# Attention scores on four 32-row groups of TensorE, with the products of two jobs in turn

## The chip, the cores and the metric

The kernel runs on one core of one Trainium2 chip. The metric is the device time of one execution in microseconds (us). All work is in one program: TensorE (PE), VectorE (DVE), ScalarE (ACT), GpSimd (POOL) and SyncE (SP, which only issues DMAs here) each run their own list in order and wait for each other through semaphores.

## The reference

A decoder layer on 16 samples of 128 tokens with 128 features, with a context of 77 tokens per sample, and a linear attention behind it:

```
x = layernorm1(x + mha(x, x, x, mask))         # 16 heads of 8 features, mask 128 x 128
x = layernorm2(x + mha(x, ctx, ctx, no mask))  # 77 keys
x = layernorm3(x + relu(x @ w1 + b1) @ w2 + b2)   # 512 hidden features
# linear attention over ctx
q, k = elu(x), elu(ctx)
x = layernorm(x + (q @ (k^T ctx)) / (q . sum(k) + 1e-6))

mha: scores = q k^T / sqrt(8); where mask == 0: -1e9; softmax over keys; times v; output projection
```

## The kernel before, in words

**Jobs and slots.** A job is one attention (self "s" or cross "c") of one sample; there are 32. Samples go in groups of two (G = 2), eight groups. `run_iterations` unrolls twelve iterations, and `iteration` has four slots k = 0 to 3 per iteration: a group's self attention jobs are at k = 0 and 1, its cross attention jobs, one iteration later, at k = 2 and 3. `schedule(i, k)` names for each slot the current job `cur`, the next one `nxt`, the previous one `prev`, and `prev_y` before that. The feed-forward part of a group runs two iterations after its self attention and the linear attention with it (`TAIL`); these and the projections are the `light_work` of a slot, placed by the table `PROJ_USES` as (name, stage, k, place), two PSUM banks in turn (`bank_of`). A bank is opened for a new use only when the last use was read (`open_bank`).

**Scores.** Queries and keys are split into a high and a low bf16 part. A head has 8 features, and 4 combinations of high and low, so 32 rows of contraction. The scores of a job are computed twice: query-major (`query_major`, L412, queries on the partitions) to find each row's maximum, and key-major (`key_major`, L439, keys on the partitions) for the exp, whose output feeds the product with the values. Each is done in two halves h of eight heads. Here two heads (JJ = 2) share 64 rows: the array `wide` holds the queries twice, each time with the other head's rows zero (the zeros are set once by two memsets on POOL, L1118). With 64 rows per instruction two row groups r = 0, 1 are in use, each with its own bank: `s1_ps[r]` for query-major, `s2_ps[r]` for key-major. A query-major half has 8 matmuls, a key-major half 4 of 256 columns. For self attention, `add_bias` (L403) first writes the mask into both banks with 4 matmuls of 64 x 64. After the key-major products, 4 matmuls subtract the maximum (L460), whose transposed bf16 parts come from `split_max` (DVE), `transpose_max` (PE) and `widen_max` (DVE, L920).

**Order around it on TensorE** (`iteration`, L650), in each slot: second half of the values product of `prev` (`times_v`, L478), `query_major(nxt, 0)`, `key_major(cur, 0)`, light work at place 0, `post_transpose_pv` of `prev` (L489), light work 1, `query_major(nxt, 1)`, `post_transpose_att` of `prev` (L494), `key_major(cur, 1)`, `post_project` of `prev` (L498), light work 2, first half of `times_v` of `cur`, `transpose_max` of `nxt`, light work 3 and 4. `blanks` are filler matmuls in the last iterations, `keep_busy` in the first.

**What it waits for.** `query_major` waits for the spreads of its rows (DMA) and, at h = 0, for the widened maximum of the job before, which shares a bank with the transposed maximum; at each half for the maxima read by DVE (`max_bank`, L904). `key_major` waits for the exp of the half before in its banks (`exp_bank`, ACT, L723). `post_transpose_att` waits for `normalise` (DVE, L934), `post_project` for ACT's copy `copy_att` (L734). ACT's order in a slot is `copy_av`, exp of bank 0, light work 0 (among it `scale_y`, L745), exp of bank 1, light work 1, `copy_att`, the two exps of half 1, light work 2 to 4. DVE's: `standardise`, two maxima, light work 0, `normalise`, light work 1, two maxima, `split_max`, `residual`, light work 2, `statistics`, `widen_max`, light work 3 and 4.

**Rows to the groups.** `spread_q_rows` (L291) issues 8 DMAs per group and kind on SP's queue (some of the last group on ACT's); `spread_k` issues 4. At the start SP also issues `late_loads` (L346) behind the first spread: inputs of the second group, the rows of biases, x, and the last weights (`w_rest`), for which TensorE waits at the start of iteration 0 (L652).

## Time and profile before

| | |
|---|---|
| runs | 295.7, 296.0, 297.46 us; median 296.0 |
| profiled execution | 296.44 us, span 294.6 us |
| granted TensorE clock, mean over the span | 0.955 |
| busy, share of the span | PE 254.7 us (86%), DVE 192.1 (65%), ACT 153.4 (52%), POOL 113.5 (39%) |
| TensorE weight loads | 159.4 us (54%), beside the matmuls |

The span is from the first to the last instruction of the program. Busy is the union of the times of an engine's instructions; matmuls are pipelined and their ends are modelled, so the start of the next instruction tells more than the duration of one. A row of the timeline is: start in us from the span's start, busy us, engine, line, operation, out<-in, shapes, count of instructions merged, and in brackets the idle time of the engine before it and what ended it. "Query-major" rows are L428, "key-major" rows L450.

### The profile page before, as it was taken

What the parts mean: (1) busy time and instruction counts of PE and PEld (TensorE: products, weight loads), DVE (VectorE), ACT (ScalarE), POOL (GpSimd) and SP (SyncE); (2) the same over time, 40 slices, a digit from 0 to 9 for tenths busy, and PEclk for the clock granted to TensorE, in tenths of its full rate; (3) what the DMA queues carried; (4) which work ended last, traced back from release to release, by engine and by line L of the source; (5) the groups of instructions that cost most, each with busy time, mean ns of one, the idle gap of its engine ahead of it and who ended that gap; (6) DMA issues with size and microseconds to landing.
All of it is one profiled execution on the core that took longest, in us unless ns stands there. A gap on an engine that the chain in (4) does not pass through costs nothing.

```text
span 294.6 us, 8333 instructions
## 1 busy us (share of the span) xinstructions
PE 254.7 (86%) x3036; PEld 159.4 (54%) x3036; DVE 192.1 (65%) x606; ACT 153.4 (52%) x374; POOL 113.5 (39%) x222
## 2 busy tenths in 40 slices
PE   8959678899998989999999999999998979779880
PEld 4424344555576557655765576557655746455540
DVE  7055355678848984898489848984898454554324
ACT  3004413565748565856585658565856563345520
POOL 5020230043224354535453545354535452632471
PEclk9997956999999999999999999999999986999998
DMA  4390111221220132012201220112010001000000
GB/s 128 93 274 7 47 49 33 75 57 44 83 59 18 33 86 76 18 33 80 79 20 36 80 77 18 36 49 80 18 36 20 19 14 37 2 29 2 0 18 19
DMA packets 28624, 14.61 MB, mean 50 GB/s; under 512 B 8024, under 2 KB 28200, under 8 KB 28584
## 3 DMA queue, kind: packets, MB, share of 16 engines
q1 hardware_dynamic: 27256, 13.48, 16.2%
q10 hardware_dynamic: 1328, 0.60, 0.7%
q8 instruction: 24, 0.39, 0.5%
q14 instruction: 16, 0.13, 0.2%
HBM read 5.46 MB, written 1.05 MB: 22 GB/s over the span
## 4 chain that ended last, share of the span: by engine, by line
PE 62%; DVE 19%; issue 6%; SPq 4%; POOL 3%; DMA 3%; ACT 2%; POOLq 0%; DVEq 0%; ACTq 0%
PE av_ps L478 10%; PE proj_ps L508 9%; DVE neg_max L904 7%; PE s_ps L408 6%; PE proj_ps L562 5%; PE s_ps L450 5%; PE s_ps L428 5%; PE post_ps L498 4%; PE s_ps L460 3%; SPq L295 3%; PE post_ps L494 3%; PE s_ps L396 3%; DMA w_sb<-in_weights 2%; DVE att L934 2%; PE proj_ps L521 2%
## 5 line engine op out<-in xcount | busy, mean ns | idle before, releaser
L723 ACT ACTIVATE probs<-s_ps 128x512 f32<-128x512 f32 (+1 forms) x128 | 72.0, 592 | 53.9 <-PE s_ps L460 53.9
L904 DVE TENSOR_REDUCE neg_max<-s_ps 128x4 f32<-128x512 f32 (+1 forms) x128 | 68.4, 576 | 36.6 <-PE s_ps L428 36.6
L1140 POOL TENSOR_SCALAR var_e<-mv 128x1 f32<-128x1 f32 x32 | 7.2, 224 | 99.9 <-DVE mv L955 99.9
L396 PE MATMUL s_ps<-zeros_b 128*128 128x512 bf16 x96 | 25.6, 398 | 1.0 <-POOL zeros_b L1115 1.0
L729 ACT COPY av_sb<-av_ps 128x256 f32<-128x256 f32 x32 | 11.7, 365 | 26.0 <-PE av_ps L478 25.9
L460 PE MATMUL s_ps<-max_x,unit_sel 64*128 64x256 bf16 (+1 forms) x256 | 25.2, 276 | 0.0
L508 PE MATMUL proj_ps<-x_t,w_sb 128*128 128x256 f32 (+1 forms) x80 | 21.8, 391 | 0.7 <-issue 0.6
L408 PE MATMUL s_ps<-bias_q,id_b 64*64 64x512 bf16 x128 | 14.2, 431 | 9.2 <-DVE neg_max L904 3.7
L1149 POOL TENSOR_TENSOR y_g<-y_n,row_sb 128x128 f32<-128x128 f32 x32 | 14.6, 458 | 17.3 <-DVE y_n L961 17.3
L478 PE MATMUL av_ps<-probs,v_aug_c 77*32 77x128 f32 x512 | 21.3, 288 | 0.0
L920 DVE TENSOR_TENSOR max_x<-s_ps,max_is_j 128x256 bf16<-128x256 bf16 x32 | 13.6, 425 | 11.4 <-PE s_ps L437 11.4
L478 PE MATMUL av_ps<-probs,v_aug_s 128*32 128x128 f32 x512 | 20.6, 279 | 0.2 <-ACT probs L723 0.2
L1142 POOL TENSOR_TENSOR rstd<-var_e,neg_half 128x1 f32<-128x1 f32 x32 | 18.2, 568 | 2.7
L494 PE MATMUL post_ps<-id_f,att 128*128 128x128 f32 x32 | 10.6, 333 | 8.3 <-DVE att L934 8.2
L745 ACT ACTIVATE x_t<-proj_ps,col_sb 128x128 f32<-128x128 f32 x32 | 14.4, 451 | 6.2 <-PE proj_ps L578 6.2
L776 ACT ACTIVATE hid<-proj_ps,col_sb 128x256 f32<-128x256 f32 (+1 forms) x32 | 12.9, 458 | 8.8 <-PE proj_ps L508 8.8
L562 PE MATMUL proj_ps<-w_sb,hid 128*128 128x128 f32 x120 | 16.6, 281 | 0.6 <-ACT hid L776 0.4
L498 PE MATMUL post_ps<-w_sb,att_t 128*128 128x128 f32 x64 | 16.1, 335 | 1.0 <-ACT att_t L734 1.0
L946 DVE TENSOR_TENSOR x_post<-post_ps,r 128x128 f32<-128x128 f32 x32 | 9.2, 288 | 11.2 <-PE post_ps L498 10.4
L562 PEld LDWEIGHTS proj_ps<-w_sb,hid 128*128 128x128 f32 x120 | 15.1, 191 | 2.5 <-ACT hid L776 2.1
L478 PEld LDWEIGHTS av_ps<-probs,v_aug_s 128*32 128x32 f32 x512 | 12.0, 109 | 6.6 <-issue 4.3
L1151 POOL TENSOR_TENSOR r<-y_g,res_bias 128x128 f32<-128x128 f32 x32 | 14.6, 456 | 2.5
(121 smaller groups left out, 505.3 us busy)
## 6 DMA issues: line engine op xcount, KB each, us to landing
xt_in<-in_x_t SPq DMA_DIRECT2D x8, 128.0 KB, 2.3
sq_wide<-sq_hi SPq DMA_DIRECT2D x32, 32.0 KB, 2.3
sq_wide<-sq_lo SPq DMA_DIRECT2D x32, 32.0 KB, 1.9
x_all<-in_x SPq DMA_DIRECT2D x8, 128.0 KB, 2.2
cq_wide<-cq_lo SPq DMA_DIRECT2D x32, 32.0 KB, 1.9
out<-o_all SPq DMA_DIRECT2D x8, 128.0 KB, 1.9
sk_rows<-sk_hi SPq DMA_DIRECT2D x14, 64.0 KB, 1.9
sk_rows<-sk_lo SPq DMA_DIRECT2D x14, 64.0 KB, 1.9
```

The lines of the kernel that those rows point to most:

```text
L396: nc.tensor.matmul(bank[:, :], zeros_b[:], zeros_b[:].unsqueeze(1).to_broadcast([P, RH, S]), start=True, stop=True, skip_group_check=True)
L408: nc.tensor.matmul(banks[r][RP * c:RP * (c + 1), :], id_b[rows, rows], bias[rows, int(c != r), :].unsqueeze(1).to_broadcast([RP, RH, S]), ...
L428: last = nc.tensor.matmul(s1_ps[r][:, at:at + n], wide[kind][rows, g % 2, jj, u, b, :], rows_k[kind][rows, g % K_COPIES[kind], u, b, :], s ...
L460: last = nc.tensor.matmul(s2_ps[r][0:n, uu * JJ * S:(uu + 1) * JJ * S], unit_sel[rows, u, 0:n], max_x[rows, b, :, :], start=False, stop=Tr ...
L478: last = nc.tensor.matmul(av_ps[32 * r:32 * r + VW, rr * S:(rr + 1) * S], v_aug[kind][:, b, u, r, :], probs[0:KLEN[kind], half, r // JJ, r ...
L494: nc.tensor.transpose(post_ps[:, 2, :], att[:, b, :], id_f[:]).then_inc(M["attt_ps"], 1)
L498: nc.tensor.matmul(post_ps[:, 3, :], att_t[:, b, :], w_sb[:, W_SO if kind == "s" else W_CO, :], start=True, stop=True).then_inc(M["o_ready ...
L508: return nc.tensor.matmul(bank[:, at:at + n], w_sb[:, w, :], src, start=True, stop=True)
L562: last = nc.tensor.matmul(bank[:, b * D:(b + 1) * D], hid[:, c, b, :], w_sb[:, W_2 + c, :], start=(c == 0 and b == first_b(i)), stop=(c == ...
L723: nc.scalar.activation(probs[0:n, h, r, :, :, :].rearrange("p u j n -> p (u j n)"), s2_ps[r][0:n, :], ACT.Exp, scale=SCALE).then_inc(M["ex ...
L904: nc.vector.tensor_reduce(neg_max[:, b, r, RH * h:RH * (h + 1)], scores, AX_X, ALU.max, negate=True).then_inc(M["max_done"], 1)
L1142: nc.gpsimd.tensor_tensor(rstd[:, b, :], var_e[:, b, :], neg_half[:, 0:1], ALU.pow).then_inc(M["rstd_ready"], 1)
```

## The change

- `rows_q` takes the place of `wide`: each head has its own 32 rows (HR = 32), there are no zero rows, no memsets on POOL and no wait for them. Weights are permuted on the host to suit (`order`).
- A spread of queries is 4 DMAs instead of 8, of 64 KB instead of 32 KB.
- A half is now 8 query-major matmuls of 32 rows (as before in number) and 8 key-major ones of 32 rows and 128 columns (4 of 64 rows and 256 columns before), and 8 matmuls of 128 columns that subtract the maximum (4 of 256 before). Half h of query-major takes row groups h and 2 + h, half h of key-major the other two.
- `score_half` opens both (waits and biases first), issues the query-major matmuls of `nxt` and the key-major ones of `cur` in turn, and then subtracts the maximum of `cur`.
- The order in TensorE's slot changes: `score_half(0)`, `post_transpose_pv`, light work 0, 1 and 2, `score_half(1)`, `post_transpose_att`, `post_project`, `times_v` of `cur`, `transpose_max`, light work 3 and 4. "la" moves from place 2 to place 3 of slot 3.
- `widen_max` is a plain copy of 128 columns instead of a product of 256.
- The sum behind the feed-forward part (L1041) moves ahead of the maxima in DVE's slot 2.
- The wait for `w_rest` moves from the start of iteration 0 to its slot 3; the first filler has 22 matmuls instead of 28.

```diff
-                for jj in range(JJ):
-                    eng.dma_start(
-                        wide[kind][4 * jj + s:P:8, g % 2, jj, :, :, :].rearrange("p u b n -> p u (b n)"),
-                        part_of(kind + "q", s)[jj * RP:(jj + 1) * RP, :, :].rearrange("p b n -> p (b n)")
-                    ).then_inc(M[f"spread_{kind}q"], 16)
+                eng.dma_start(rows_q[kind][s:P:4, g % 2, :, :, :].rearrange("p u b n -> p u (b n)"),
+                              part_of(kind + "q", s)[:].rearrange("p b n -> p (b n)")).then_inc(
+                    M[f"spread_{kind}q"], 16)
...
+            def head_rows(r, odd):
+
+                return slice(HR * (2 * r + odd), HR * (2 * r + odd + 1))
+
+            def open_query_major(kind, b, g, job, h):
+
                 if h == 0:
                     wait_spread(pe, kind + "q", g)
                     wait_spread(pe, kind + "k", g)
...
                 wait_reuse(pe, M["max_done"], job * UNITS + RG * h)
                 if kind == "s":
                     add_bias(s1_ps, bias_q)
+
+            def open_key_major(kind, b, g, job, h):
+
+                wait_reuse(pe, M["exp_done"], job * UNITS + RG * h)
+                if kind == "s":
+                    add_bias(s2_ps, bias_k)
+
+            def query_major(kind, b, g, job, h, u, r):
+
+                n = KLEN[kind]
+                rows = head_rows(r, h)
+                last = nc.tensor.matmul(s1_ps[r][:, u * n:(u + 1) * n], rows_q[kind][rows, g % 2, u, b, :],
+                                        rows_k[kind][rows, g % K_COPIES[kind], u, b, :],
+                                        start=(kind == "c"), stop=True, skip_group_check=True)
+                if u == UNITS - 1:
+                    last.then_inc(M["s1_ready"], 1)
+
+            def key_major(kind, b, g, job, h, u, r):
+
+                rows = head_rows(r, 1 - h)
+                nc.tensor.matmul(s2_ps[r][0:KLEN[kind], u * S:(u + 1) * S], rows_k[kind][rows, g % K_COPIES[kind], u, b, :],
+                                 rows_q[kind][rows, g % 2, u, b, :],
+                                 start=(kind == "c" and u == 0), stop=False, skip_group_check=True)
+
+            def subtract_max(kind, b, g, job, h):
+
+                if h == 0:
+                    pe.wait_ge(M["maxt_ready"], job + 1)
+                for u in range(UNITS):
+                    for r in range(RG):
+                        rows = head_rows(r, 1 - h)
+                        last = nc.tensor.matmul(s2_ps[r][0:KLEN[kind], u * S:(u + 1) * S],
+                                                unit_sel[rows, u, 0:KLEN[kind]], max_x[rows, b, :],
+                                                start=False, stop=True, skip_group_check=True)
+                        if u == UNITS - 1:
+                            last.then_inc(M["s2_ready"], 1)
+
+            def score_half(nxt, cur, h):
+
+                if nxt:
+                    open_query_major(*nxt, h)
+                if cur:
+                    open_key_major(*cur, h)
+                for u in range(UNITS):
+                    for r in range(RG):
+                        if nxt:
+                            query_major(*nxt, h, u, r)
+                        if cur:
+                            key_major(*cur, h, u, r)
+                if cur:
+                    subtract_max(*cur, h)
...
             def iteration(i):
-                if static(i) and i == SELF:
-                    pe.wait_ge(M["w_rest"], 16)
                 for k in range(4):
+                    if static(i) and (i, k) == (SELF, 3):
+                        pe.wait_ge(M["w_rest"], 16)
                     cur, nxt, prev, _ = schedule(i, k)
                     if static(i) and i == NEXT and k == 3:
...
-                        keep_busy(28)
+                        keep_busy(22)
                     if prev:
                         times_v(i, *prev, 1)
                     blanks(i, k, "scores")
-                    if nxt:
-                        query_major(*nxt, 0)
-                    if cur:
-                        key_major(*cur, 0)
-                    blanks(i, k, "y")
-                    light_work(i, k, 0)
+                    score_half(nxt, cur, 0)
                     blanks(i, k, "pv")
                     if prev:
                         post_transpose_pv(*prev)
+                    blanks(i, k, "y")
+                    light_work(i, k, 0)
                     light_work(i, k, 1)
...
-                    if nxt:
-                        query_major(*nxt, 1)
+                    light_work(i, k, 2)
+                    score_half(nxt, cur, 1)
...
                     if prev:
                         post_transpose_att(*prev)
-                    if cur:
-                        key_major(*cur, 1)
                     blanks(i, k, "proj")
                     if prev:
                         post_project(*prev)
...
-                    light_work(i, k, 2)
                     if cur:
                         times_v(i, *cur, 0)
...
-                nc.vector.tensor_tensor(max_x[:, b, :, :], nmt_ps.unsqueeze(1).to_broadcast([P, JJ, S]),
-                                        max_is_j[:].unsqueeze(2).to_broadcast([P, JJ, S]), ALU.mult).then_inc(
-                    M["maxt_ready"], 1)
+                nc.vector.tensor_copy(max_x[:, b, :], nmt_ps).then_inc(M["maxt_ready"], 1)
```

## Rows read from the trace of the kernel before

**Rows 1.** The page, the chain that ended last by line.

```profile
PE av_ps L478 10%; PE proj_ps L508 9%; DVE neg_max L904 7%; PE s_ps L408 6%; PE proj_ps L562 5%; PE s_ps L450 5%; PE s_ps L428 5%; PE post_ps L498 4%; PE s_ps L460 3%; SPq L295 3%; PE post_ps L494 3%; PE s_ps L396 3%; DMA w_sb<-in_weights 2%; DVE att L934 2%; PE proj_ps L521 2%
```

**Rows 2.** Stretches: one round in four slots; busy us by engine, granted clock.

```profile
128.92:136.64 7.72, 7.08 (x95) 4.19 (x96) 6.50 (x23) 4.80 (x13) 3.04 (x8) 1.00 0.17 51
136.64:145.85 9.21, 8.71 (x105) 6.04 (x105) 5.65 (x17) 4.89 (x12) 6.34 (x11) 1.00 0.26 73
145.85:151.89 6.04, 5.58 (x88) 3.96 (x85) 5.22 (x20) 4.71 (x12) 1.63 (x4) 1.00 0.14 41
151.89:158.32 6.43, 5.91 (x90) 3.87 (x86) 5.78 (x16) 4.35 (x12) 2.93 (x7) 1.00 0.15 39
```

**Rows 3.** Timeline, TensorE, first score half of slot 0: start, busy, instruction, count.

```profile
128.92 0.41 PE L408 MATMUL s_ps<-bias_q,id_b 64*64 64x512 bf16 x4
129.27 0.40 PE L428 MATMUL s_ps<-sk_rows,sq_wide 64*128 64x128 bf16 x8
129.59 0.41 PE L408 MATMUL s_ps<-bias_k,id_b 64*64 64x512 bf16 x4
129.94 0.39 PE L450 MATMUL s_ps<-sq_wide,sk_rows 64*128 64x256 bf16 x4
130.16 0.38 PE L460 MATMUL s_ps<-max_x,unit_sel 64*128 64x256 bf16 x4
130.48 0.33 PE L578 MATMUL proj_ps<-id_f,y_n 128*128 128x128 f32 x1
```

**Rows 4.** Timeline, TensorE, slot 2: first score half and what follows.

```profile
145.85 0.32 PE L428 MATMUL s_ps<-ck_rows,cq_wide 64*128 64x77 bf16 x8
...
146.53 0.33 PE L578 MATMUL proj_ps<-id_f,y_n 128*128 128x128 f32 x1
```

**Rows 5.** Timeline, TensorE, an early slot: transpose and output projection.

```profile
35.79 0.33 PE L494 MATMUL post_ps<-id_f,att 128*128 128x128 f32 x1 [0.68 <-DVE att L934]
...
36.47 0.80 PE L498 MATMUL post_ps<-w_sb,att_t 128*128 128x128 f32 x2 [0.36 <-ACT att_t L734]
```

**Rows 6.** Timeline, VectorE: two widenings, and second maxima of slots 2 and 3.

```profile
128.24 0.42 DVE L920 TENSOR_TENSOR max_x<-s_ps,max_is_j 128x256 bf16<-128x256 bf16 x1
...
135.96 0.42 DVE L920 TENSOR_TENSOR max_x<-s_ps,max_is_j 128x256 bf16<-128x256 bf16 x1 [0.70 <-PE s_ps L437]
...
148.54 0.83 DVE L904 TENSOR_REDUCE neg_max<-s_ps 128x4 f32<-128x308 f32 x2
...
155.15 1.28 DVE L904 TENSOR_REDUCE neg_max<-s_ps 128x4 f32<-128x512 f32 x2
```

**Rows 7.** Groups by line, VectorE: count, busy us, mean ns of one.

```profile
L911 DVE CAST nm_parts<-neg_max 128x16 bf16<-128x16 f32 x32 | 7.7, 241 | 1.1
```

**Rows 8.** Timeline, ScalarE and TensorE, slot 1.

```profile
137.87 0.60 ACT L723 ACTIVATE probs<-s_ps 128x512 f32<-128x512 f32 x1 [0.81 <-PE s_ps L460]
...
138.37 0.45 ACT L745 ACTIVATE x_t<-proj_ps,col_sb 128x128 f32<-128x128 f32 x1
...
140.24 0.49 PE L498 MATMUL post_ps<-w_sb,att_t 128*128 128x128 f32 x2
...
140.57 1.03 PE L508 MATMUL proj_ps<-x_t,w_sb 128*128 128x256 f32 x4
```

**Rows 9.** Timeline of the start.

```profile
7.37 6.21 PE L396 MATMUL s_ps<-zeros_b 128*128 128x512 bf16 x28
...
10.20 2.51 SPq L295 DMA_DIRECT2D sq_wide<-sq_lo  x4
...
14.06 0.41 PE L408 MATMUL s_ps<-bias_q,id_b 64*64 64x512 bf16 x4 [0.48 <-DMA sq_wide<-sq_lo]
...
18.98 0.43 DVE L920 TENSOR_TENSOR max_x<-s_ps,max_is_j 128x256 bf16<-128x256 bf16 x1 [0.32 <-PE s_ps L437]
...
21.61 0.41 PE L408 MATMUL s_ps<-bias_q,id_b 64*64 64x512 bf16 x4 [2.66 <-DMA w_sb<-in_weights]
```

**Rows 10.** Stretches: an early one at the lower clock.

```profile
38.00:44.00 6.00, 4.55 (x30) 1.92 (x29) 3.23 (x7) 1.18 (x4) 2.39 (x5) 0.50 0.15 37
```

More of the change, by code:

```diff
@@ L162, in decoder_layer_kernel @@
         cn_in = sb("cn_in", [SK, G, D + 1])
-        hi, lo, rows_k, wide = {}, {}, {}, {}
+        hi, lo, rows_k, rows_q = {}, {}, {}, {}
         for kind in "sc":
@@ L263, in wait_spread @@
         def wait_spread(eng, key, g):
[L265 removed]
+            eng.wait_ge(M["spread_" + key], 16 * 4 * (g + 1))
         def part_of(key, s):
@@ L421, in query_major @@
                     add_bias(s1_ps, bias_q)
-                for uu in range(2):
-                    u = 2 * h + uu
-                    for jj in range(JJ):
-                        for r in range(RG):
-                            rows = slice(RP * r, RP * (r + 1))
-                            at = (uu * JJ + jj) * n
-                            last = nc.tensor.matmul(s1_ps[r][:, at:at + n], wide[kind][rows, g % 2, jj, u, b, :],
-                                                    rows_k[kind][rows, g % K_COPIES[kind], u, b, :],
-                                                    start=(kind == "c"), stop=True, skip_group_check=True)
-                            if uu == 1 and jj == JJ - 1:
-                                last.then_inc(M["s1_ready"], 1)
+            def open_key_major(kind, b, g, job, h):
+                wait_reuse(pe, M["exp_done"], job * UNITS + RG * h)
+                if kind == "s":
+                    add_bias(s2_ps, bias_k)
@@ L474, in times_v @@
                 pe.wait_ge(M["exp_done"], job * UNITS + RG * (half + 1))
-                for u in (2 * half, 2 * half + 1):
-                    a, rr = u // 2, u % 2
-                    for r in range(RH):
-                        last = nc.tensor.matmul(av_ps[32 * r:32 * r + VW, rr * S:(rr + 1) * S],
-                                                v_aug[kind][:, b, u, r, :],
-                                                probs[0:KLEN[kind], half, r // JJ, rr, r % JJ, :],
-                                                start=(u == 0), stop=(a == 1), skip_group_check=True)
+                for r in range(RG):
+                    for u in range(UNITS):
+                        last = nc.tensor.matmul(av_ps[32 * u:32 * u + VW, r * S:(r + 1) * S],
+                                                v_aug[kind][:, b, 2 * half + r, u, :],
+                                                probs[0:KLEN[kind], half, r, u, :],
+                                                start=(half == 0 and r == 0), stop=(half == 1), skip_group_check=True)
                 last.then_inc(M["av_ready"], 1)
@@ L1116, in _ @@
             nc.gpsimd.memset(neg_half[:], -0.5).then_inc(M["half_set"], 1)
-            for kind in "sc":
-                nc.gpsimd.memset(wide[kind][:].rearrange("p a j u b n -> p (a j u b n)").bitcast(F32), 0.0).then_inc(
-                    M["wide_clear"], 1)
             pool.wait_ge(M["half_set"], 1)
```

66 lines of the change are left out of this document (18 added, 48 removed).

## The prediction

> **What bounds the kernel now.** I read the page first: the chain that ended last is spread over a dozen TensorE lines and the row maximum of VectorE, with no line above 10% [rows 1]. So no single wait is there to remove, and busy shares will not do; the question is what paces one round of the steady state. The table of stretches cuts one round into its four slots, each from one opening of the query-major product to the next [rows 2]: 7.72, 9.21, 6.04 and 6.43 us, 29.40 together. I call them slots 0 to 3. Seven such rounds lie between 39 and 246 us. TensorE works 27.3 of the 29.4 us by the same rows, VectorE 23.2, ScalarE 18.8. Then I read the order of work inside the slots, engine by engine, for what each engine waits on.
>
> **Scores on TensorE.** In slot 0 (both jobs self attention) the first score half starts at 128.92 and ends at 130.48, 1.56 us [rows 3]: bias 0.35, query-major 0.32, bias 0.35, key-major 0.22, maximum 0.31 (starts to next starts). Key-major is 4 instructions of 256 columns, two at a time over two row groups: 2 x 256 columns at 2.4 GHz are 0.213 us, so it streams at full rate. Bias is 512 columns in four quadrants at once, 0.213 of its 0.35; query-major is 4 x 128 columns deep, 0.213 of its 0.32. The remaining 0.14 and 0.11 lie where the next instruction has another tile shape.
>
> After the change the two biases stand together (0.21 + 0.35), and 16 products of 128 columns run on four row groups: four deep, 0.22 if all four run at once. They have the shape of the maximum behind them (8 instructions on two row groups, 4 deep, 0.32 with the change of shape that follows). The half costs 0.56 + 0.22 + 0.32 = 1.10 us, 0.46 less. Where one of the two jobs is cross attention, one bias goes: 0.35 + 0.22 + 0.32 = 0.89, against 1.13 (0.25 for the narrower query-major, the rest as above; estimate from rows 3 and 4). Both cross: 0.54 against 0.68 [rows 4]. Second halves gain as much or up to 0.1 more, since each of the two parts was entered by itself. Per round: 0.92 + 0.48 + 0.40 + 0.59 = 2.4 us of TensorE work goes. The bounds of the unknown term, 16 products in 0.22: nothing in this trace runs four row groups at once. If only two overlap, as key-major does now, it is 0.44; that end stays for the range, and 0.22 is taken because quadrants of the bias already overlap four-fold. The Trainium skill, "TensorE: Matmul & The Clock Gate", section on packing small matmuls, gives a measured 3.07 times for four row tiles; by that the term would be 0.28 and TensorE would lose 0.5 us of its gain per round. No row here shows it.
>
> **A new wait.** The second key-major half used to stand between the transpose of the attention output and the output projection, and hid ScalarE's copy. Now the projection comes straight behind the transpose. Where the trace has that already, the projection starts 0.68 us after the transpose, with TensorE idle 0.36 [rows 5]. So each slot gets 0.36 us of stall, 1.4 per round. Queued behind it are the first half of the values product and the transpose of the maxima. Against that, the transpose's own wait for VectorE's normalised output (0.68 in the same rows) is now covered by the projections and the second half moved ahead of it.
>
> **What paces each slot then.** TensorE's balance, 2.4 less 1.4, would suggest 1 us, but the slots end by other queues.
> Slot 0: from one widened maximum to the next VectorE takes 7.72 us, of which it is idle 0.70 [rows 6]; 7.02 is its own list. The widening is now a plain copy of half the size: 0.24 by the mean of the cast [rows 7] against 0.42, a gain of 0.1 to 0.18. TensorE's own list is 7.08 of busy time [rows 2] less 0.92 plus 0.36, 6.5. So VectorE sets the slot: 6.9, a gain of 0.8.
> Slot 1: the first up-projection now has to come before the second half, and it waits for ScalarE's scaled y, which is queued behind an exp. ScalarE's exp and its y take 0.50 + 0.45 [rows 8]; scores 0.89 + 0.1 + 0.95 gives 2.0, up-projection 0.95, second half 0.89, copy wait 0.68, projection 0.33: 4.85. Before, from 136.64 to 140.24, projection 0.33 and up-projection about 0.95, it was 4.88 [rows 8]. The rest is unchanged: no gain.
> Slot 2: the second maximum starts 2.69 after the opening now [rows 6]; after, the second half starts when exp of the first is out (0.54 + 0.1 + 0.50 + 0.45 + 0.6, 2.2), and its query-major is done 0.4 later: 2.6, as good as now. What follows on VectorE is the same but for the copy: gain 0.1 to 0.2, I take 0.2. The feed-forward sum, moved ahead of the maxima, frees a bank earlier for the context product; it ends a TensorE stall that the wait for exp then takes over, so nothing more. If it were late, it would hold the maxima of its slot by its own 0.4.
> Slot 3: VectorE starts the second maximum at 3.26 [rows 6], at the end of its list and not of a wait; gain 0.1 to 0.2. The linear attention product, moved behind the transpose of the maxima, is read by VectorE only after the widening, so it delays nobody; its 0.5 us of TensorE are moved, not added.
> Sum per round 0.8 + 0 + 0.2 + 0.15 = 1.15, about 1.2; seven rounds 8.4 us.
>
> **The start.** Eight spreads of queries (the row shows the last four, at 10.20) hold the first scores to 14.06, behind a DMA [rows 9]. Half as many issues at 0.63 end 2.5 us earlier; then the filler holds it, which starts at 7.37 and has 22 instead of 28 matmuls of 0.22 [rows 9]: it ends at 12.2, a gain of 1.8. The next opening waited from 19.4, when the maxima were widened, for the last weights, until 21.61 [rows 9]. That wait moves to slot 3, where these weights are first used; they are also issued 2.5 earlier. The opening comes at about 17.5, a gain of 4.1, the 1.8 in it. The rows of biases, issued 2.5 us earlier, land just in time (bound: up to 0.5 late). The following slot gains about 1 more, because its projection is ahead of its second half and the engine had restarted after an idle time at the lower clock. I take 5; bounds 3.5 and 7. POOL's two big memsets and their wait are nothing: they end before the first spread. The four spreads a time in later rounds were ahead of their use; nothing.
>
> **The end.** After 246 us the slots are chains of latency with filler in between. The new stall (0.36) and the saved scores cancel: 0, bounds minus 2 and plus 3.
>
> Sum: 5 + 8.4 = 13.4. The profiled execution took 296.44 us with a span of 294.6; the median of the runs is 296.0, within 0.2%. 296.44 - 13.4 = **283 us**. Its own range is 279 to 289 (start and end 3.5 less or more, a round 0.9 to 1.5).
>
> **Rivals.**
> (a) Better: the waits for exp and VectorE shrink as their inputs come earlier, and a round gains most of TensorE's 2.4 less part of the stalls, 2.1: 5 + 15 = 20, **276 us**. For it, VectorE and ScalarE have over 3 us of idle time in slot 1 [rows 2]. Against it, slot 0 has none to give. 15%.
> (b) The products do not do what they say: two row groups at a time. Eight halves a round at 0.22 more are 1.8, of which half falls into waits: a round gains 0.3, and the whole 7: **289 to 291 us**. For it, only two-way overlap has been seen with 128 wide outputs. 7%.
> (c) Reading the banks paces the round altogether: exp and maximum of the first half must be out before the second half of both jobs opens, in every slot, and the 8 reads of 0.6 us a slot and what is queued among them keep each slot as long as now. Only the start is gained: **291 us**. The Trainium skill says this of tiling, "TensorEngine Tiling (Array Packing)", section "PSUM Bottleneck": packing speeds TensorE but not the emptying of its banks. The trace half agrees, since VectorE's list is 7.02 of slot 0, but leaves it 3.6 us idle in slot 1 [rows 2]. 10%.
> (d) Slower: the clock. TensorE gets a stall in every slot, and four-fold packing means less streaming time for the same work. From 38 to 44 us it was busy 4.55 of 6 us at granted clock 0.50, the level of 1.2 GHz, while the rounds at 90% and more have 1.00 [rows 2, 10]. After the change a round is busy about 24.9 of 28.2, 88%. If slot 3, with its wait for exp, fell to the lower level in each round, its 5 us of TensorE work would grow by more than half, some 3 us a round: 21 in all, **304 us**. It decides the sign from 13.4 / 7 = 1.9 us a round. Against it, the rounds stay far above that 76%. 8%.
>
> **Chances.** Forecast 60%, (a) 15, (b) 7, (c) 10, (d) 8. A difference under 1% (293 to 299) is what a measurement here can't tell from none. (a) and the forecast are faster; of (b) and (c), spread around 290, about half lands in the same band: faster 0.83, same 0.09, slower 0.08. Range 276 to 292: it leaves out (d), and the tails of (a) and (c).
>
> **What would show it.** The score halves of slot 0 at 1.1 us on TensorE, the 16 products at 0.22 (0.44 for (b)); an idle time near 0.36 before the projection, put down to ScalarE's copy; slot 0 near 6.9 us with VectorE without idle time; slot 1 unchanged near 9.2; the second opening at about 17.5 us; the clock at 1.00 in the rounds. A round under 27.5 us speaks for (a), near 29.4 for (b) or (c), and a clock below 0.9 inside the rounds for (d). The step I trust least is slot 1's wait for the scaled y.

## The result, and the profile after

| | before | changed |
|---|---|---|
| median of the runs | 296.57 us (295.7 to 297.46) | 309.09 us (306.25 to 314.17) |
| profiled execution, span | 296.44, 294.6 us | 314.17, 312.2 us |
| granted TensorE clock, mean | 0.955 | 0.880 (0.899 to 0.927 in the other runs) |
| TensorE busy | 254.7 us, 86% | 258.9 us, 83% |

The changed kernel is slower: ratio 1.034, interval 1.029 to 1.039. The prediction said 283.0, in 276 to 292. The execution shown here is the one with the most time at the low clock; the ratios, here and below, compare only runs with little of it, three of 306 to 307 us here, and by the medians this one would be 1.042.

From the page of the changed kernel: the granted clock in 40 slices of 7.8 us, in tenths, then the chain that ended last by engine and by line.

```profile
PEclk9996558555699999999999999999999955897997
...
PE 67%; ACT 10%; issue 9%; DVE 8%; POOL 3%; DMA 1%; SPq 1%; POOLq 0%; ACTq 0%; DVEq 0%
```

The reader is to see two things. The clock row is low from the fourth to the eleventh slice, up to 83 us, where the kernel before was back at full clock after 50 us, and again from 250 to 265 us, where the kernel before had a shorter dip. And VectorE, 19% of the chain before, is at 8%; ScalarE and TensorE's own issue took its place. TensorE waits for ScalarE now.

One round between openings of the first score half, with the same columns as [rows 2], and two stretches at the lower clock. The slots 3, 0, 1 and 2 come in this order, since the round is cut where no filler or low clock disturbs it.

```profile
132.57:139.44 6.87, 5.60 (x105) 3.54 (x101) 5.21 (x16) 4.21 (x11) 3.21 (x7) 1.00 0.16 38
139.44:146.64 7.20, 6.38 (x116) 3.94 (x112) 6.03 (x22) 4.47 (x13) 2.24 (x5) 1.00 0.31 86
146.64:156.03 9.39, 8.40 (x119) 6.02 (x119) 5.53 (x18) 4.84 (x12) 7.10 (x13) 1.00 0.26 72
156.03:162.27 6.24, 5.53 (x106) 4.03 (x102) 4.79 (x19) 4.37 (x12) 1.29 (x4) 1.00 0.01 4
56.00:68.00 12.00, 10.65 (x128) 7.34 (x128) 5.96 (x21) 5.00 (x13) 2.43 (x6) 0.50 0.10 29
68.00:80.00 12.00, 11.05 (x138) 6.05 (x131) 5.91 (x16) 3.90 (x10) 3.31 (x8) 0.50 0.14 33
```

Slots 0 to 3 take 7.20, 9.39, 6.24 and 6.87 us, 29.70 together, against 7.72, 9.21, 6.04 and 6.43 of [rows 2] and 6.9, 9.2, 5.84 and 6.28 predicted. All four are longer than predicted; against the kernel before, slot 0 is shorter and the other three are longer. TensorE's busy time did shrink, from 27.3 to 25.9 us a round; its idle time grew from 2.1 to 3.8. Two other stretches of the kernel before, to set beside 56 to 80 us:

```profile
56.00:68.00 12.00, 10.77 (x165) 6.78 (x167) 8.77 (x28) 7.23 (x19) 3.39 (x8) 1.00 0.20 54
68.00:80.00 12.00, 11.44 (x171) 6.83 (x167) 9.80 (x29) 7.79 (x21) 4.07 (x9) 1.00 0.23 65
```

TensorE was as busy there, 10.77 and 11.44 of 12 us, at clock 1.00; the changed kernel's 10.65 and 11.05 are at 0.50. It did less in that time, 128 and 138 instructions against 165 and 171: at 0.50 the same work keeps the engine busy for longer.

TensorE of the changed kernel, in slot 3 and then in slot 0, the latter to set beside [rows 3] and [rows 5]. Of the products, which follow in more rows, only the first row stands.

```profile
134.15 0.27 PE L588 MATMUL proj_ps<-id_f,y_n 128*128 128x128 f32 x1
135.01 0.67 PE L518 MATMUL proj_ps<-x_t,w_sb 128*128 128x256 f32 x2 [0.59 <-ACT x_t L749]
...
139.44 0.41 PE L403 MATMUL s_ps<-bias_q,id_b 64*64 64x512 bf16 x4
...
140.00 0.23 PE L431 MATMUL s_ps<-sk_rows,sq_rows 32*128 32x128 bf16 x1
...
140.24 0.39 PE L451 MATMUL s_ps<-max_x,unit_sel 32*128 32x128 bf16 x8
140.56 0.44 PE L499 MATMUL post_ps<-id_f,av_sb 128*128 128x128 f32 x2
140.83 0.27 PE L588 MATMUL proj_ps<-id_f,y_n 128*128 128x128 f32 x1
...
141.75 1.10 PE L518 MATMUL proj_ps<-xt_in,w_sb 128*128 128x256 f32 x4 [0.21 <-ACT x_t L749]
142.78 0.41 PE L403 MATMUL s_ps<-bias_q,id_b 64*64 64x512 bf16 x4
...
143.89 0.33 PE L504 MATMUL post_ps<-id_f,att 128*128 128x128 f32 x1
144.58 0.49 PE L508 MATMUL post_ps<-w_sb,att_t 128*128 128x128 f32 x2 [0.35 <-ACT att_t L738]
```

VectorE's two pairs of maxima in slot 0, of the changed kernel and then of the kernel before:

```profile
140.52 1.28 DVE L906 TENSOR_REDUCE neg_max<-s_ps 128x4 f32<-128x512 f32 x2
...
143.76 1.29 DVE L906 TENSOR_REDUCE neg_max<-s_ps 128x4 f32<-128x512 f32 x2 [0.75 <-PE s_ps L431]
```

```profile
130.14 1.28 DVE L904 TENSOR_REDUCE neg_max<-s_ps 128x4 f32<-128x512 f32 x2
...
132.55 1.28 DVE L904 TENSOR_REDUCE neg_max<-s_ps 128x4 f32<-128x512 f32 x2
```

### The profile page after: what moved, and what is told of

Its sections match the earlier page's. It is cut to its first block, busy times and chain, and to the rows that moved or that the text cites. A ratio compares the mean times of both kernels' runs of the same rounds, so it can differ in the third digit from the quotient of the medians.

```text
span 312.2 us, 9289 instructions
## 1 busy us (share of the span) xinstructions
PE 258.9 (83%) x3542; PEld 166.5 (53%) x3542; DVE 181.5 (58%) x605; ACT 147.9 (47%) x374; POOL 109.5 (35%) x220
## 4 chain that ended last, share of the span: by engine, by line
PE 67%; ACT 10%; issue 9%; DVE 8%; POOL 3%; DMA 1%; SPq 1%; POOLq 0%; ACTq 0%; DVEq 0%
PE proj_ps L518 10%; PE av_ps L488 10%; PE s_ps L403 6%; PE post_ps L508 5%; PE proj_ps L572 5%; PE s_ps L431 5%; PE s_ps L451 4%; PE s_ps L391 4%; PE proj_ps L531 3%; ACT x_t L749 3%; DVE neg_max L906 3%; PE post_ps L499 3%; PE s_ps L440 3%; PE post_ps L504 3%; ACT att_t L738 3%
## 5 line engine op out<-in xcount | busy, mean ns | idle before, releaser
L738 ACT COPY att_t<-post_ps 128x128 f32<-128x128 f32 x32 | 8.5, 265 | 52.8 <-PE post_ps L504 52.8
L518 PE MATMUL proj_ps<-x_t,w_sb 128*128 128x256 f32 (+1 forms) x80 | 24.0, 420 | 9.5 <-issue 4.8
L451 PE MATMUL s_ps<-max_x,unit_sel 32*128 32x128 bf16 (+1 forms) x512 | 27.1, 227 | 0.0
L508 PE MATMUL post_ps<-w_sb,att_t 128*128 128x128 f32 x64 | 17.5, 359 | 11.3 <-ACT att_t L738 11.3
L488 PE MATMUL av_ps<-probs,v_aug_c 77*32 77x128 f32 x512 | 23.2, 305 | 0.0
L488 PE MATMUL av_ps<-probs,v_aug_s 128*32 128x128 f32 x512 | 22.1, 296 | 0.0
L518 PEld LDWEIGHTS proj_ps<-x_t,w_sb 128*128 128x128 f32 x80 | 13.8, 203 | 13.9 <-ACT x_t L749 6.8
L508 PEld LDWEIGHTS post_ps<-w_sb,att_t 128*128 128x128 f32 x64 | 10.7, 211 | 18.7 <-ACT att_t L738 18.7
L451 PEld LDWEIGHTS s_ps<-max_x,unit_sel 32*128 32x128 bf16 (+1 forms) x512 | 19.7, 112 | 0.0
L962 DVE TENSOR_SCALAR y_n<-x_post,mv,rstd 128x128 f32<-128x128 f32 x32 | 11.0, 344 | 13.6 <-POOL rstd L1141 13.2
L499 PE MATMUL post_ps<-id_f,av_sb 128*128 128x128 f32 x64 | 15.6, 330 | 2.8 <-ACT av_sb L733 2.8
```

Source lines behind the costliest of these rows:

```text
L451: last = nc.tensor.matmul(s2_ps[r][0:KLEN[kind], u * S:(u + 1) * S], unit_sel[rows, u, 0:KLEN[kind]], max_x[rows, b, :], start=False, stop ...
L488: last = nc.tensor.matmul(av_ps[32 * u:32 * u + VW, r * S:(r + 1) * S], v_aug[kind][:, b, 2 * half + r, u, :], probs[0:KLEN[kind], half, r ...
L499: last = nc.tensor.transpose(post_ps[:, rr, :], av_sb[:, b, rr * S:(rr + 1) * S], id_f[:])
L508: nc.tensor.matmul(post_ps[:, 3, :], att_t[:, b, :], w_sb[:, W_SO if kind == "s" else W_CO, :], start=True, stop=True).then_inc(M["o_ready ...
L518: return nc.tensor.matmul(bank[:, at:at + n], w_sb[:, w, :], src, start=True, stop=True)
```

## The experiments

All are compared with the kernel before in runs beside them (medians 295.7, 295.0 and 296.3 us in the three batches). A round is measured in the profiled execution, from one widened maximum of slot 3 to the next; with that measure it is 29.40 before and 29.70 in the changed kernel. "The changed kernel's order" is its order of TensorE's slot. The edits are shown shortened, by their main lines.

**Two factors apart: rows per head, and order.** The first run keeps the 32 rows and all else of the change, and gives TensorE the order of before, the y transpose and "la" included; its second halves are two separate loops.

```diff
-light_work(i, k, 2); score_half(nxt, cur, 1)
+query_half(nxt, 1)
 post_transpose_att(*prev)
+key_half(cur, 1)
 post_project(*prev)
+light_work(i, k, 2)
```

> The changed kernel with TensorE's order of the kernel before: y transposed ahead of the values transposes, second half apart (query-major, attention transpose, key-major), output projection behind key-major, light work 2 behind it, la at its old place. Rows of 32, first half in turns, starts as changed. Theory 1 (the order made it slower: y to scaled y to projection in a row, the bare copy wait, and through the thinner TensorE work the low clock of the first 80 us): below 292 us, a round of 28.0 to 28.8, low clock only up to about 50 us. Theory 2 (the four-fold packing itself keeps the clock low, the order is innocent): 300 us or more, low clock again from 56 to 83 us, round near 29.5.

Measured: median 290.0 us (284.5 to 291.4). Two widened maxima, one round apart, 28.11 us:

```profile
121.16 0.23 DVE L939 COPY max_x<-s_ps 128x128 bf16<-128x128 bf16 x1 [0.34 <-PE s_ps L490]
...
149.27 0.23 DVE L939 COPY max_x<-s_ps 128x128 bf16<-128x128 bf16 x1 [0.34 <-PE s_ps L490]
```

The opposite corner: the kernel before, 64 rows and all, with nothing but the new order (again the y transpose and "la" too).

```diff
+light_work(i, k, 2)
 query_major(*nxt, 1)
+key_major(*cur, 1)
 post_transpose_att(*prev)
-key_major(*cur, 1)
 post_project(*prev)
-light_work(i, k, 2)
```

> The kernel before (64 rows, eight spreads, starts and VectorE's list as before) with TensorE's new order alone: values transposes ahead of y, light work 2 ahead of the second half, key-major 1 straight behind query-major 1, then attention transpose and projection, la in place 3. Theory 1 (the order costs about 1.6 us a round whatever the rows): a round 31.0 to 31.8 against 29.4, 308 to 316 us. If the order only hurts together with the packing and turns, 297 to 301.

Measured: 317.6 us, ratio 1.078 (1.073 to 1.082). The two widenings:

```profile
138.05 0.42 DVE L920 TENSOR_TENSOR max_x<-s_ps,max_is_j 128x256 bf16<-128x256 bf16 x1
...
169.77 0.42 DVE L920 TENSOR_TENSOR max_x<-s_ps,max_is_j 128x256 bf16<-128x256 bf16 x1
```

The round is 31.72, and the mean clock of the runs, 0.957 to 0.963, is that of the kernel before. So the clock has no part in this one. The four corners:

| us a round (median) | order of before | new order |
|---|---|---|
| 64 rows | 29.40 (296.6) | 31.72 (317.6) |
| 32 rows | 28.11 (290.0) | 29.70 (309.1) |

The 32 rows, with all that came with them but the order (the plain copy of the maxima, the moved sum, the start), are worth 1.3 to 2.0 us a round, and the order costs 1.6 to 2.3. So in the rounds the whole loss of the change lies in its order. The clock divides otherwise. With 64 rows the runs have mean clocks of 0.950 to 0.966 in the order of before and 0.957 to 0.963 in the new one; with 32 rows 0.912 to 0.944 and 0.880 to 0.927. The low clock comes with the 32 rows or with something that came with them, in either order, and there is most of it in the new one.

**Which part of the order.** Turns first: all query-major matmuls of a half, then all key-major ones.

```diff
-for u, r: query_major(...); key_major(...)
+for u, r: query_major(...)
+for u, r: key_major(...)
```

> The changed kernel with the query-major and key-major products of a half one after the other instead of in turns; all else as changed. If turns give what they should (0.22 us of the 0.44), each half with both jobs is 0.2 longer on TensorE, but three of four second halves end waits of ScalarE or VectorE: a round 0.5 to 1.5 us longer, 309 to 315 us. If the four-fold packing is what lowers the clock (theory 2), less low clock and the same or a shorter time, 300 to 306. Theory 1 expects no help for the clock.

Measured: 302.7 us, ratio 1.023 (1.016 to 1.030), round 29.83. Turns are worth 0.13 us a round, not 0.5 to 1.5, and the rows of TensorE say why (query-major is L431, key-major L440; rows between are left out):

```profile
130.18 0.23 PE L431 MATMUL s_ps<-sk_rows,sq_rows 32*128 32x128 bf16 x2
130.20 0.23 PE L440 MATMUL s_ps<-sq_rows,sk_rows 32*128 32x128 bf16 x2
...
130.35 0.22 PE L431 MATMUL s_ps<-sk_rows,sq_rows 32*128 32x128 bf16 x2
```

All eight query-major products stand ahead of the key-major ones in the program, and yet the first key-major products start at 130.20, before the last query-major ones at 130.35. The maximum behind them starts at 130.44, so the 16 products take 0.26 us against 0.24 in turns: the four row groups overlap either way, and this run does not take the packing away.

The median is lower than that of the changed kernel, and the clock of its runs higher (0.925 to 0.942 against 0.880 to 0.927). A shorter time without turns was what I expected if the packing itself kept the clock low. But the packing was still there, so the run can't say that; why its clock stayed higher is open.

The y transpose (light work 0) ahead of the values transposes, as before the change, the rest as changed:

```diff
+light_work(i, k, 0)
 post_transpose_pv(*prev)
-light_work(i, k, 0)
```

> The changed kernel with y transposed (light work 0) ahead of the values transposes, as before the change. Theory 1: the scaled y comes 0.4 earlier in slots 0, 1 and 3, where a projection waits for it ahead of the second half: slot 3 0.3 to 0.4 shorter, slots 0 and 1 0.1 to 0.2, a round 29.0 to 29.2 instead of 29.7, 301 to 304 us. Theory 2: 306, no change beyond 1 us.

Measured: 303.1 us (298.5 to 305.8), ratio 1.015 (1.005 to 1.025), round 29.43: 0.27 us less, nearly all of it in slot 3. Its clocks spread from 0.904 to 0.942, and in its profiled execution, as in that of e2_no_turns, the stretch from 40 to 80 us has 0.91, where the changed kernel's has 0.59.

Cover for ScalarE's copy: the first half of the values product moves between the transpose and the projection.

```diff
 post_transpose_att(*prev)
+times_v(i, *cur, 0)
 post_project(*prev)
-times_v(i, *cur, 0)
```

> The changed kernel with the first half of the values product between the attention transpose and the output projection, which covers ScalarE's copy. Theory 1: the 0.36 us stalls of TensorE go, 1.4 us a round on TensorE, half of it taken back by VectorE's residual, which comes 0.3 later: a round 28.8 to 29.2, 300 to 304 us. Theory 2: 305 to 307.

A miss: 317.6 us (311.6 to 318.4). The one round that kept the full clock takes 29.64, no less than without the cover (29.70): as long as the second half is late, covering the copy gains nothing. VectorE's two pairs of maxima in slot 0 are 3.24 us apart here too (200.77 and 204.01). What did change was the clock, in the middle of the rounds. Its stretches:

```profile
85.30:99.00 13.70, 12.11 (x156) 7.92 (x155) 8.88 (x30) 7.96 (x21) 4.06 (x8) 0.70 0.08 21
99.00:103.00 4.00, 4.00 (x54) 2.35 (x53) 2.81 (x11) 0.67 (x2) 2.37 (x5) 0.50 0.17 49
```

A mean of 0.70, and then 0.50 with TensorE busy all of 4.00 us. The rounds with such a stretch take 31.6 to 34.1.

**The light work behind the second half.** Now light work 2 covers the copy instead of standing ahead of the second half (with the y transpose first):

```diff
-light_work(i, k, 2)
 score_half(nxt, cur, 1)
 post_transpose_att(*prev)
+light_work(i, k, 2)
 post_project(*prev)
```

> The changed kernel with y first and light work 2 moved from ahead of the second half to between the attention transpose and the projection; the second half stays in turns. If the place of light work 2 is what costs (half 1 waiting for a projection that waits for the scaled y, and the bare copy), a round 28.0 to 28.5 instead of 29.4, 288 to 294 us. If the merging of the second half is what costs (query-major held back by exp), a round stays above 29.

Measured: 287.7 us (286.2 to 288.4), ratio 0.976 (0.970 to 0.983). Its round in slots 3, 0, 1, 2:

```profile
144.91:151.03 6.12, 5.58 (x105) 3.50 (x101) 5.21 (x16) 4.12 (x11) 3.22 (x7) 1.00 0.17 41
151.03:157.38 6.35, 6.10 (x115) 4.03 (x112) 5.94 (x22) 4.45 (x13) 2.23 (x5) 1.00 0.36 99
157.38:166.55 9.17, 8.07 (x123) 6.08 (x122) 6.04 (x18) 4.86 (x12) 7.11 (x13) 1.00 0.26 73
166.55:172.46 5.91, 5.08 (x103) 3.93 (x99) 4.79 (x19) 4.36 (x12) 1.28 (x4) 1.00 0.00 0
```

27.55 us in all. In slot 0 the second half opens 2.42 us after the first, against 3.34 (139.44 to 142.78) in the changed kernel, and the projections of the next group stand in the copy's stall. TensorE, then VectorE's two pairs of maxima:

```profile
154.66 0.33 PE L504 MATMUL post_ps<-id_f,att 128*128 128x128 f32 x1
154.82 1.04 PE L518 MATMUL proj_ps<-xt_in,w_sb 128*128 128x256 f32 x4
155.69 0.39 PE L508 MATMUL post_ps<-w_sb,att_t 128*128 128x128 f32 x2
```

```profile
152.11 1.28 DVE L906 TENSOR_REDUCE neg_max<-s_ps 128x4 f32<-128x512 f32 x2
...
154.52 1.28 DVE L906 TENSOR_REDUCE neg_max<-s_ps 128x4 f32<-128x512 f32 x2
```

The pairs start 2.41 us apart; in the changed kernel 3.24. Against e3_y_first this one move is 29.43 - 27.56 = 1.87 us a round. It does two things at once, though: the second half no longer waits behind the light work, and the copy is covered. TensorE is busy 24.8 us a round here, so this order shows the whole 2.4 us of work that I expected to go; in the changed kernel the same instructions add up to 25.9, more of them behind a wait (the projections at 141.75 have 1.10 on record, those at 154.82 here 1.04).

The same, but with light work 2 behind the projection, so that the copy stays bare:

```diff
 score_half(nxt, cur, 1)
 post_transpose_att(*prev)
-light_work(i, k, 2)
 post_project(*prev)
+light_work(i, k, 2)
```

> As e6, but light work 2 behind the output projection instead of between it and the attention transpose: the copy wait of 0.36 is bare again, while the second half still waits for no projection. Against the round of 29.4 of e3 (light work 2 ahead of the second half) and 27.56 of e6: if the place ahead of the second half was nearly all of the loss, 27.8 to 28.5; if the bare copy wait is a full term of 1.4 us a round, 28.9 to 29.2. Time 288 to 296 us.

A miss again: 310.6 us (304.4 to 313.9), round 30.8. Its slots 0, 2 and 3, between openings as above, have the full clock, and can be set beside those of e6_light2_cover:

```profile
129.97:136.85 6.88, 6.29 (x116) 3.92 (x113) 6.01 (x21) 4.56 (x13) 2.48 (x6) 1.00 0.32 90
148.00:154.17 6.17, 5.14 (x103) 3.90 (x99) 4.87 (x19) 4.48 (x12) 1.62 (x4) 1.00 0.01 4
154.17:160.72 6.55, 5.66 (x105) 3.50 (x101) 5.85 (x17) 4.23 (x11) 3.04 (x7) 1.00 0.16 39
```

The three slots take 19.60 us; in e3_y_first, with the light work ahead of the second half and the copy bare, 20.04 (7.20, 6.22 and 6.62), and in e6_light2_cover, 18.38. So to free the second half alone gives 0.4 us, and to cover the copy then gives 1.2 more, without any help of the clock. In e4_cover_copy the same cover gave nothing. Each delay hides the other, and only with both gone is the slot short. What VectorE waits for before the widening of the maxima over the whole run (us, count, longest) shows the change of place, in e9_light2_behind and then in e6_light2_cover:

```profile
DVE max_x L923 <- PE s_ps L475: 17.1, 23, 1.9
```

```profile
DVE max_x L923 <- PE s_ps L475: 3.0, 7, 1.1
```

In e3_y_first that wait is 1.7 us, and the wait of the maxima for their products 36.9; here they are 17.1 and 23.3. In slot 0 the two pairs of maxima are 2.48 us apart (130.96 and 133.44), nearly as in the kernel before, and yet VectorE then waits 0.41 us for the transposed maxima, which stand on TensorE behind the bare stall and the projections.

The other 2.0 us a round lie in slot 1, with the clock. TensorE in slot 1, and the clock around it:

```profile
77.81 0.41 PE L403 MATMUL s_ps<-bias_k,id_b 64*64 64x512 bf16 x4 [1.13 <-ACT probs L727]
...
79.39 0.79 PE L508 MATMUL post_ps<-w_sb,att_t 128*128 128x128 f32 x2 [0.35 <-ACT att_t L738]
```

```profile
75.10:78.50 3.40, 2.27 (x63) 1.37 (x57) 2.52 (x8) 2.17 (x6) 1.12 (x3) 1.00 0.19 54
78.50:82.00 3.50, 3.15 (x21) 2.02 (x19) 1.98 (x7) 1.32 (x4) 0.70 (x2) 0.59 0.31 83
```

TensorE waits 1.13 us for exp and 0.35 for the copy within 2 us, is busy 2.27 of 3.40, and in the next stretch the clock is 0.59, here and 30.7 us later again, in every round. With the light work as cover (above), the wait for exp is there too (0.98 to 1.00) and the clock holds in all but two of the rounds. So two gaps close together went ahead of each fall here. That the second gap is what brings it is not shown: e4_cover_copy has the copy covered and falls all the same.

And the covered version with no turns:

```diff
-for u, r: query_major(...); key_major(...)
+for u, r: query_major(...)
+for u, r: key_major(...)
```

> As e6, with query-major and key-major of a half one after the other. Turns save TensorE 0.2 us in 6 halves and 0.1 in 2 of a round, 1.4 in all. In the order of e6 TensorE and VectorE share the bound: a round 0.3 to 1.0 longer than 27.56, 290 to 295 us. If less than 0.15 longer, the packing pays by the saved changes of tile shape and not by the turns.

Measured: 290.4 us (285.2 to 294.4), ratio 0.967 (0.955 to 0.978), round 27.65 against 27.56. Turns are worth 0.09; here too the two jobs' products overlap without them (16 in 0.26 us, from 128.53 to 128.79).

**The start and its clock.** Filler matmuls in the waits of the first iteration, on the changed kernel, on the old order with 32 rows, and on the covered version. The edit is a table of counts by slot and place; two more stand in slot 0 of iteration 1.

For the changed kernel:

```diff
+EARLY_BLANKS = {(1, "mid"): 4, (1, "proj"): 1, (2, "pv"): 3, (2, "y"): 2, (2, "mid"): 3, (2, "proj"): 1,
+                (2, "end"): 2, (3, "y"): 3, (3, "mid"): 2, (3, "tm"): 6}
```

> The changed kernel with filler matmuls in TensorE's waits of iteration 0 and one in iteration 1. It prices the low clock of the start in the changed kernel: rounds unchanged at 29.7; if the low clock up to 83 us comes from the waits of that stretch, it shrinks to under 20 us in all before 100 us and the time is 298 to 303 us. If the low clock comes from the packing and not the waits, it falls again at 56 us and the time stays at 306 or above.

For the old order:

```diff
+EARLY_BLANKS = {(1, "att"): 3, (2, "y"): 4, (2, "att"): 3, (2, "proj"): 1, (2, "end"): 1,
+                (3, "y"): 2, (3, "mid"): 3, (3, "tm"): 3}
```

> The old order with the rows of 32 (as e1) and filler in TensorE's waits of iteration 0. Rounds 28.1 as in e1, low clock before 60 us from 17 to under 7 us, 280 to 286 us; without the filler 284 to 291. If the filler delays what it stands before, it gives nothing, 290.

For the covered version:

```diff
+EARLY_BLANKS = {(1, "mid"): 3, (1, "proj"): 1, (2, "y"): 5, (2, "att"): 2,
+                (2, "end"): 2, (3, "y"): 4, (3, "mid"): 2, (3, "tm"): 2}
```

> As e6, with filler in TensorE's waits of iteration 0 and one in iteration 1. Rounds 27.56; the low clock of about 14 us before 60 us goes below 7: 283 to 287 us. If the fillers only move the low clock elsewhere, 287 to 289.

Changed kernel with filler: 307.4 us (300.6 to 309.1). Old order with filler: 287.7 (284.0 to 292.0), ratio 0.969 (0.960 to 0.977). Covered version with filler: **282.9 us** (281.5 to 288.3), ratio 0.954 (0.946 to 0.963), better than both kernels. The runs of one kernel give an estimate of the price of the clock. With filler the changed kernel took 307.41 us at mean clock 0.921 and 300.58 at 0.955, with no other difference on record; in time at the lower level that is 48 and 27 us ((1 - clock) x 2 x span), so about 0.33 us for each. The old order gives 0.40 (292.03 at 0.929, 283.96 at 0.962), but the changed kernel without filler only 0.26 (314.17 at 0.880, 306.25 at 0.927).

The filler did not do for the changed kernel what I expected if the waits of the start alone made the low clock (298 to 303 us): the clock fell again from 52 us and the median stayed above 306, which I had both put down as signs for the packing. Like the four corners, this leaves the packing as a suspect. It can't be all of it: e6_light2_cover and the covered version with filler have the same products in the same turns, and mean clocks of 0.938 to 0.942 and 0.927 to 0.965. The first 80 us of the covered version with filler, then 40 to 80 us of the changed kernel:

```profile
0.00:40.00 40.00, 34.19 (x328) 16.91 (x328) 19.65 (x56) 11.50 (x27) 6.12 (x18) 1.00 0.39 110
40.00:80.00 40.00, 34.57 (x641) 23.64 (x635) 26.52 (x80) 22.86 (x57) 9.13 (x21) 0.96 0.24 65
```

```profile
40.00:80.00 40.00, 33.49 (x437) 19.89 (x436) 19.86 (x57) 14.15 (x35) 5.75 (x13) 0.59 0.15 40
```

Last, the start alone, on the kernel before: the wait for the last weights moves from the start of iteration 0 to its slot 3.

```diff
-if static(i) and i == SELF: pe.wait_ge(M["w_rest"], 16)
 for k in range(4):
+    if static(i) and (i, k) == (SELF, 3): pe.wait_ge(M["w_rest"], 16)
```

> The kernel before with one edit: the wait for the last weights at slot 3 of iteration 0 instead of its start. The maxima of job 1 are widened at 25.5 to 26 us instead of 28.1, 2.2 from the DMA and the rest from the clock, and the whole is 2 to 3 us shorter, 292 to 294 us. If later waits take it back, 295 to 296.

Measured: 294.7 us in ten runs, ratio 0.995 (0.991 to 0.999), barely apart from none. The second opening comes earlier by 1.63 us than in [rows 9]:

```profile
19.98 0.41 PE L408 MATMUL s_ps<-bias_q,id_b 64*64 64x512 bf16 x4 [0.72 <-DVE max_x L920]
```

Job 1's widened maximum is at 25.6 us, 2.5 earlier; at the end 1.6 of it is left by the medians (294.7 against 296.3).

## Why the prediction was wrong

**Right: the products.** Slot 0's first half runs from 139.44 to 140.56, 1.12 us against the 1.10 predicted. Its 16 products start in four bundles from 140.00 on, and the maximum behind them at 140.24: 0.24 against 0.22, where two at a time would be 0.44. So the four row groups run at once and rival (b) fell. The Trainium skill, "TensorE: Matmul & The Clock Gate", section on packing small matmuls, has 3.07 times for four row tiles of 512 columns, by which the products would take 0.28, an estimate. The trace's 0.24, at 128 columns, lies between that and the 0.21 of four times.

**Right: the start.** Filler, first and second opening of the changed kernel:

```profile
7.49 4.91 PE L391 MATMUL s_ps<-zeros_b 128*128 128x512 bf16 x22
12.33 0.41 PE L403 MATMUL s_ps<-bias_q,id_b 64*64 64x512 bf16 x4
...
17.73 0.41 PE L403 MATMUL s_ps<-bias_q,id_b 64*64 64x512 bf16 x4 [0.52 <-DVE max_x L923]
```

12.33 and 17.73 against 12.2 and 17.5 predicted. Job 1's widened maximum came at 23.1 us, 28.1 before: the 5 us were there. By job 6 (77.0 against 70.1) they were gone, and more.

**Right in size, wrong in effect: the copy.** The projection starts 0.69 us after the transpose with 0.35 idle (143.89, 144.58). I charged 1.4 us a round against TensorE's gain, and then nothing in the slots, since VectorE was to set them. Covering it gave nothing in the changed kernel's order (e4_cover_copy), and 1.2 us in three slots once the second half was free (e6_light2_cover against e9_light2_behind). Over the profiled execution the wait adds up to 11.3 us in 31 times (us, count, longest):

```profile
PE post_ps L508 <- ACT att_t L738: 11.3, 31, 0.5
```

**The failed step: "What paces each slot then".** I took each slot as the longer of two separate lists, TensorE's and VectorE's. I let slot 1 alone pay for light work 2 standing ahead of the second half, and priced that at nothing; the copy's stall I let vanish behind VectorE. In fact each slot pays, because the engines wait for each other in a row. TensorE transposes y, ScalarE scales it, then TensorE runs the projections of light work 2, and only then opens the second half; exp and the maxima of that half wait behind all of it. In slots 1 and 3 the projections read the scaled y. In slots 0 and 2 they do not, but they take the PSUM bank that the transpose used, and wait 0.2 us until ScalarE has read it (141.75).

In slot 0 I said that VectorE would have no idle time and set the slot at 6.9. It waits 0.75 us for the query-major products (143.76), its pairs of maxima start 3.24 us apart, 2.41 before (130.14 and 132.55), and the slot takes 7.20. In slot 3 I expected the second maxima to depend on the end of VectorE's list. The y transpose, behind the values transposes and their wait for ScalarE, starts at 134.15, the projection at 135.01 after 0.59 of idle time, and the second products at 135.96, 3.39 after the opening: slot 3 takes 6.87 instead of 6.3. In slot 2 the same, 6.24 instead of 5.84. The term of the sum was 0.8 + 0 + 0.2 + 0.15 = 1.15 a round in favour, and measured 0.30 against: over seven rounds some 10 us.

That the order is the cause is shown from both sides: alone on the kernel before it costs 2.3 us a round at an unchanged clock (e5_before_new_order), and undone in its light work 2 it gives 1.87 back (e6_light2_cover). That it takes two delays at once, the late second half and the bare copy, is shown by the runs that take away one: 29.64 a round with only the copy covered, 0.4 us in three slots with only the second half freed. Even VectorE's own list was not the 6.9 that I took as a floor: in e6_light2_cover slot 0 takes 6.35. Rival (c), reading the banks as the pace, is no cause either, since e6_light2_cover reads them as often in 27.56.

**Rival (d), at 8%, was too low and in the wrong place.** I looked for the low clock in slot 3 of the steady rounds. There the clock stayed at 1.00. In the profiled execution it fell in the first 83 us and around 250 to 265. By the clock of each run the changed kernel is 44 to 75 us at the lower level, the kernel before about 20 to 30. A run at 0.911 has 54, some 29 more than before, and at 0.33 us each (e7_fill's runs) these are worth 9.6 us. The 10.4 us that such a run loses (306.98 against 296.57) then add up roughly, as an estimate: 9.6 of clock, 1.5 of the five rounds behind job 8, 1.8 at the end, where from job 31's widened maximum on it takes 32.4 against 30.6 us (I had put 0, with a bound of 3), and 3.9 that the order costs between jobs 1 and 6 (its size in e5_before_new_order, where the clock differs little), less the 5.0 of the start: 11.8. The clock's price is the loosest term; at 0.26 us each the clock is 7.5 and the sum 9.7.

**Point by point.** Halves at 1.1 and products at 0.22: right. Idle near 0.36 before the projection: right. Slot 0 near 6.9 with VectorE never idle: wrong. Slot 1 near 9.2: 9.39. Second opening near 17.5: right. Clock 1.00 in the rounds: right, and not enough. A round under 27.5 for (a), near 29.4 for (b) or (c): 29.70, by neither's mechanism. "The step I trust least is slot 1's wait for the scaled y": near the failed step, but slot 1 lost only 0.2 us, and slots 0 and 3 missed by more.

**What stays open.** Why the clock stays low from 56 to 80 us with TensorE busy about 90%, why the runs of e2_no_turns and e3_y_first have less of it in rounds of nearly the same length, and why e4_cover_copy falls inside its rounds while e6_light2_cover does so in only two, is not settled. Two gaps in quick succession go ahead of each fall in e9_light2_behind, and filler in the first iteration shortens the low time without ending it: e7_fill has 1.00 up to 40 us and 0.70 from there to 80. Whether the four-fold packing keeps the clock low, as rival (d) had it, is not settled either: the kernels with 64 rows have the high clock in both orders, but packing, plain copy and start change together between them, and only the start was tried alone (e12_before_start: 0.961 to 0.972 in eight of ten runs). No run varies the gaps by themselves.

## What to carry to other kernels

When two jobs' work is merged into one block, ask what has to be ahead of it now: everything queued before the second half delays that half's exp and maxima by its own waits, whatever TensorE saves inside the block. Put work that others don't wait for behind the block, in the stall of a copy. Do not price a slot as the longest of separate lists: follow the chain through all engines to the end of the slot. Two delays can hide each other, so that taking away either alone shows next to nothing (e4_cover_copy, e9_light2_behind) and both together pay (e6_light2_cover); one experiment that gains nothing does not prove that a stall is free. Give the clock a term of its own with wide bounds when a change adds or moves idle time; here runs of one kernel lay 7 to 8 us apart with nothing else on record between them, and the clock could not be told from the gaps.

## What the runs showed of the hardware

- 16 matmuls of 32 rows and 128 columns, alternating over four row groups, start in bundles of four about 60 ns apart: 0.24 us for all, weight loads included.
- The overlap does not need the program's turns: with eight query-major products ahead of eight key-major ones, the latter start before the last of the former (130.20 and 130.35 in e2_no_turns), and the 16 take 0.26 us. Turns were worth 0.09 to 0.13 us a round of eight halves.
- The lower clock can last 24 us and more with TensorE busy 10.65 and 11.05 of 12 us. By pairs of runs of one kernel, a us at the lower level went with 0.26 to 0.40 us of time, an estimate; a kernel bound by TensorE alone would pay half a us.
- The same kernel can get quite different amounts of the low clock: the changed kernel's five runs have mean clocks from 0.880 to 0.927.
- With a stall taken away (e4_cover_copy) the clock fell to 0.50 inside the rounds, which went from 29.6 to 34 us; with it left bare in another order (e9_light2_behind) it fell to 0.59 for one stretch in each round.
